# Two changes of order in the softmax pipeline of a windowed-attention stage: the row maximum ahead of the row sum on VectorE, and later slots for the steps behind

## The chip, the cores and the metric

The kernel runs on the 8 cores of one Trainium2 chip. Every core does the same work on its own 2048 tokens; nothing passes between cores. The time is that of the slowest core, in device microseconds (us).

## What is computed

One "macaron" layer on x of 16384 tokens by 1024 features: half a mixture-of-experts block, windowed attention, half a mixture-of-experts block again. The change lies in the attention.

```python
x = x + 0.5 * ffn(layernorm(x))          # shared MLP + 15 experts, top 3 of them weighted
x = x + attn(layernorm(x))
x = x + 0.5 * ffn(layernorm(x))

# attn: 16 heads of 64, chunks of 64 queries
q, k, v = x @ Wq.T + bq, x @ Wk.T + bk, x @ Wv.T + bv
k3, v3 = (chunk before, own chunk, chunk after)
scores = einsum('bnqhd,bnkhd->bhnqk', qc, k3) / sqrt(64)
band = (rel >= -32) & (rel <= 32)        # rel: key position less query position
attn = softmax(where(band & inside, scores, -inf))
out  = einsum('bhnqk,bnkhd->bnqhd', attn, v3).reshape(b, s, d) @ Wo.T + bo
```

The dense reference mixture is computed as written: every expert runs on every token, and the weights of the experts that a token did not pick are zero.

## The kernel before

Each core holds its 2048 tokens and 64 more on either side, feature-major, in `R` (fp32), with the normalised copy in `zT` (bf16). The stages follow one another: layer norm, feed-forward, layer norm, attention, layer norm, feed-forward.

The attention (`phase_attn`) handles four quarters of 512 queries each. A quarter has three parts:

1. The projections K, V and Q, as 128x512 and 128x128 matmuls from `zT` and weights in the two buffers `wA` and `wB`. The weights come by four DMAs of 2 MB on GpSimd's queue (line 731).
2. The softmax loop, 16 iterations j: four blocks of 128 queries by four groups of four heads.
3. The output projection (line 1032, weights in `wB`) and its addition to `R` (line 1044). It starts when the last context copy of the loop is done.

Within the softmax loop one iteration goes through eight steps. The names in the right column are those used from here on.

| step | engine, lines | what | name |
|---|---|---|---|
| 1 | TensorE 869 to 885 | mask by an identity matmul, then scores of 4 heads over 256 keys, into the pair of PSUM banks `pQ[j % 2]` | S(j) |
| 2 | VectorE 946, 948, 951 | negated row maximum from the two banks, then the smaller of the two | max(j) |
| 3 | ScalarE 1005, 1007 | exp with the maximum as bias, PSUM to `esc[j % 2]` | exp(j) |
| 4 | VectorE 932, 934, 937 | row sums of `esc`, reciprocal | sum(j) |
| 5 | GpSimd 969 | `atb = esc * rec` | mul(j) |
| 6 | TensorE 896, 897 | 8 transposes of `atb` into PSUM | T(j) |
| 7 | ScalarE 986 | copy of the transposed block to SBUF | cpT(j) |
| 8 | TensorE 913, 916 and ScalarE 994 | context matmuls, and their copy to `ctxT` | C(j), cpC(j) |

The order is written out by hand. Every engine runs its own queue over slots i = 0, 1, 2, ...; in slot i it does the steps that are listed for it, in this order. A step whose j lies outside 0 to 15 becomes a drain and an empty instruction that still counts the semaphore up, so that every slot adds the same number.

| engine | slot i before |
|---|---|
| TensorE | S(i), T(i-2), C(i-3) |
| VectorE | sum(i-1), max(i) |
| GpSimd | mul(i-1) |
| ScalarE | cpT(i-2), cpC(i-3), exp(i) |

There are 19 slots (`NC2 = NIT + 3`). The functions `pe_s`, `pe_t`, `pe_c`, `d1`, `d2`, `g_n`, `a1`, `a2`, `a3` give the semaphore count at which a step of iteration j is done (`d1` the maximum, `d2` the sum, `g_n` the multiplication, `a1` the exp, `a2` and `a3` the two copies). All buffers of the loop are double: S(j) waits for exp(j-2), exp(j) waits for mul(j-2) and sum(j-2), mul(j) for T(j-2), T(j) for cpT(j-2), C(j) for cpC(j-2).

Of the kernel before, what the change touches and what calls it, by code (L numbers as in the profile page):

```python
# [8 lines left out]
BF16 = mybir.dt.bfloat16  # L9
# [4 lines left out]
P = 128  # L14
# [31 lines left out]
def build_program(upto=99, taps=(), aq=4, anit=16, aout=True, acut=99):  # L46
# [49 lines left out]
    with es:  # L96
# [578 lines left out]
        def phase_attn():  # L675
            uid[0] += 1
            u = uid[0]
            with ExitStack() as ps:
# [9 lines left out]
                vbuf = ps.enter_context(nc.sbuf_tensor(f"at_v{u}", [P, 5, D], BF16))  # L688
                qTb = ps.enter_context(nc.sbuf_tensor(f"at_qT{u}", [P, DC, 512], BF16))
                ctxT = ps.enter_context(nc.sbuf_tensor(f"at_cT{u}", [P, DC, 512], BF16))  # L690
                esc = [ps.enter_context(nc.sbuf_tensor(f"at_es{i}{u}", [P, 4, 256], BF16)) for i in range(2)]
                nmx2 = [ps.enter_context(nc.sbuf_tensor(f"at_n2{i}{u}", [P, 2], F32)) for i in range(2)]
                atb = [ps.enter_context(nc.sbuf_tensor(f"at_ab{i}{u}", [P, 4, 256], BF16)) for i in range(2)]
                atT = [ps.enter_context(nc.sbuf_tensor(f"at_aT{i}{u}", [P, 8, P], BF16)) for i in range(2)]
# [11 lines left out]
                for qh in range(aq):  # L706
# [121 lines left out]
                        return pe1 + 3 * j + 1  # L828

                    def pe_t(j):  # L830
                        return pe1 + 3 * (j + 2) + 2

                    def pe_c(j):
                        return pe1 + 3 * (j + 3) + 3

                    def d2(j):
                        return dve1 + 2 * (j + 1) + 1

                    def d1(j):
                        return dve1 + 2 * j + 2  # L840

                    def g_n(j):
                        return gp1 + j + 2

                    def a2(j):
                        return act1 + 3 * (j + 2) + 1

                    def a3(j):
                        return act1 + 3 * (j + 3) + 2

                    def a1(j):
                        return act1 + 3 * j + 3

                    NC2 = NIT + 3
                    act1v, dve1v = s_act.n, s_dve.n

                    if True:
                        @blk.tensor
                        def _(t):
                            t.wait_ge(s_act.h, act1v)  # L860
                            t.wait_ge(s_dve.h, dve1v)
                            for i in range(NC2):
# [23 lines left out]
                                else:  # L886
                                    t.drain()
                                    t.nop().then_inc(s_pe.h, 1)
                                if 0 <= i - 2 < NIT:
                                    j = i - 2  # L890
                                    t.wait_ge(s_gp.h, g_n(j))
                                    if j >= 2:
                                        t.wait_ge(s_act.h, a2(j - 2))
                                    pT = pT2[j % 2]
                                    for sidx in range(4):
                                        t.transpose(pT[:, 2 * sidx, :], atb[j % 2][:, sidx, 0:128], identb[:, :])  # L896
                                        mm = t.transpose(pT[:, 2 * sidx + 1, :], atb[j % 2][:, sidx, 128:256], identb[:, :])
                                        if sidx == 3:
                                            mm.then_inc(s_pe.h, 1)
                                else:  # L900
                                    t.drain()
                                    t.nop().then_inc(s_pe.h, 1)
                                if 0 <= i - 3 < NIT:
                                    j = i - 3
                                    pl, hq = divmod(j, 4)
                                    t.wait_ge(s_act.h, a2(j))
                                    if j >= 2:
                                        t.wait_ge(s_act.h, a3(j - 2))
                                    pC = pC2[j % 2]
                                    for sidx, e in enumerate((0, 2, 1, 3)):  # L910
                                        h = 4 * hq + e
                                        hp = h % 2
                                        t.matmul(pC[hp * HD:(hp + 1) * HD, e // 2, :],
                                                 vbuf[:, pl, h * HD:(h + 1) * HD],
                                                 atT[j % 2][:, 2 * sidx, :], start=True, stop=False)
                                        mm = t.matmul(pC[hp * HD:(hp + 1) * HD, e // 2, :],
                                                      vbuf[:, pl + 1, h * HD:(h + 1) * HD],
                                                      atT[j % 2][:, 2 * sidx + 1, :], start=False, stop=True)
                                        if sidx == 3:
                                            mm.then_inc(s_pe.h, 1)  # L920
                                else:
                                    t.drain()
                                    t.nop().then_inc(s_pe.h, 1)
                        s_pe.n += 3 * NC2

                        @blk.vector
                        def _(v):
                            for i in range(NC2):
                                if 0 <= i - 1 < NIT:
                                    j = i - 1  # L930
                                    v.wait_ge(s_act.h, a1(j))
                                    v.tensor_reduce(out=sro[j % 2][:, 0:2], in_=esc[j % 2][:, 0:2, :],
                                                    axis=AX.X, op=ALU.add)
                                    v.tensor_reduce(out=sro[j % 2][:, 2:4], in_=esc[j % 2][:, 2:4, :],
                                                    axis=AX.X, op=ALU.add)
                                    v.drain()
                                    v.reciprocal(rec[j % 2][:, :], sro[j % 2][:, :])
                                    v.drain()
                                    v.nop().then_inc(s_dve.h, 1)  # L939
                                else:  # L940
                                    v.drain()
                                    v.nop().then_inc(s_dve.h, 1)
                                if 0 <= i < NIT:
                                    j = i
                                    v.wait_ge(s_pe.h, pe_s(j))
                                    v.tensor_reduce(out=nmx2[j % 2][:, 0:1], in_=pQ[j % 2][0][:, :],
                                                    axis=AX.X, op=ALU.max, negate=True)
                                    v.tensor_reduce(out=nmx2[j % 2][:, 1:2], in_=pQ[j % 2][1][:, :],
                                                    axis=AX.X, op=ALU.max, negate=True)
                                    v.drain()  # L950
                                    v.tensor_reduce(out=nmx[j % 2][:, 0:1], in_=nmx2[j % 2][:, :],
                                                    axis=AX.X, op=ALU.min)
                                    v.drain()
                                    v.nop().then_inc(s_dve.h, 1)
                                else:
                                    v.drain()
                                    v.nop().then_inc(s_dve.h, 1)
                        s_dve.n += 2 * NC2

                        @blk.gpsimd  # L960
                        def _(g):
                            for i in range(NC2):
                                if 0 <= i - 1 < NIT:
                                    j = i - 1
                                    g.wait_ge(s_dve.h, d2(j))
                                    if j >= 2:
                                        g.wait_ge(s_pe.h, pe_t(j - 2))
                                    b_ap = rec[j % 2][:, :].unsqueeze(2).broadcast_to((P, 4, 256))
                                    g.tensor_tensor(out=atb[j % 2][:, :, :], in0=esc[j % 2][:, :, :],  # L969
                                                    in1=b_ap, op=ALU.mult)  # L970
                                    g.drain()
                                    g.nop().then_inc(s_gp.h, 1)  # L972
# [5 lines left out]
                        @blk.scalar  # L978
                        def _(s):
                            for i in range(NC2):  # L980
                                if 0 <= i - 2 < NIT:
                                    j = i - 2
                                    s.wait_ge(s_pe.h, pe_t(j))
                                    if j >= 2:
                                        s.wait_ge(s_pe.h, pe_c(j - 2))
# [1 line left out]
                                else:  # L987
                                    s.drain()
                                    s.nop().then_inc(s_act.h, 1)
                                if 0 <= i - 3 < NIT:  # L990
                                    j = i - 3
                                    pl, hq = divmod(j, 4)
                                    s.wait_ge(s_pe.h, pe_c(j))
                                    s.copy(ctxT[:, 2 * hq:2 * hq + 2, pl * P:(pl + 1) * P],
# [4 lines left out]
                                if 0 <= i < NIT:  # L999
                                    j = i  # L1000
                                    s.wait_ge(s_dve.h, d1(j))
                                    if j >= 2:
                                        s.wait_ge(s_gp.h, g_n(j - 2))
                                        s.wait_ge(s_dve.h, d2(j - 2))
                                    s.activation(esc[j % 2][:, 0:2, :], pQ[j % 2][0][:, :],
                                                 AF.Exp, bias=nmx[j % 2][:, 0:1])
                                    s.activation(esc[j % 2][:, 2:4, :], pQ[j % 2][1][:, :],
                                                 AF.Exp, bias=nmx[j % 2][:, 0:1]).then_inc(s_act.h, 1)
                                else:
                                    s.drain()  # L1010
# [157 lines left out]
```

## Time and profile before

| | us |
|---|---|
| median of 4 runs | 5416.4 |
| lowest and highest of them | 4871.3, 5500.51 |
| the profiled execution | 4869.68 |
| its span, first to last instruction of the slowest core (core 7) | 4867.8 |
| spans of the eight cores | 4854.0 to 4867.8 |

| engine | busy us | share of the span |
|---|---|---|
| PE, TensorE matmul | 4264.8 | 88% |
| DVE, VectorE | 1522.2 | 31% |
| ACT, ScalarE | 879.5 | 18% |
| POOL, GpSimd | 281.1 | 6% |

The profile comes from one execution on the slowest core. A view of groups gives, for each line and engine, the count, the busy time and the idle time before it with the instruction that ended it. The timeline gives single instructions: start in us from the span's start, length in us, engine (PEld is the weight load of TensorE), line, operation, output and inputs, and in brackets the idle time before it and what ended it. A "q" behind an engine's name is that engine's instruction queue. The TensorE clock is given as a share of 2.4 GHz, so 0.50 is 1.2 GHz.

### The profile page before, as it was taken

Reading aid. Unit: us, or ns where it says so; the run is one execution under the profiler, and the core shown is the slowest. Engines: PE = TensorE matmul, PEld = TensorE weight load, DVE = VectorE, ACT = ScalarE, POOL = GpSimd, SP = SyncE. Lnnn points to the kernel's source line nnn. Section 1 sums busy time; section 2 is a strip of 40 time slices with the busy share of each in tenths; the row PEclk is TensorE's granted clock in tenths of the full one; section 3 lists DMA queues with packets and bytes.
Section 4 is the critical chain, followed back from the end, with each engine's and each line's share of the span. In section 5 each row is a group of like instructions: output and inputs, shape, how many; then the busy total and the mean of one; then the engine's idle time right before and its main releaser. Section 6 shows DMA issues by size and latency. Waiting matters only on the chain. (4 is left out here: it accounts for less than half of the span.)

```text
span 4867.8 us, 55255 instructions; the slowest of 8 cores (4854.0 to 4867.8 us)
## 1 busy us (share of the span) xinstructions
PE 4264.8 (88%) x21809; PEld 1983.2 (41%) x21809; DVE 1522.2 (31%) x1740; ACT 879.5 (18%) x932; POOL 281.1 (6%) x183
## 2 busy tenths in 40 slices
PE   1399999999999999953777761899999999999998
PEld 0144444444444444421333330344444444444444
DVE  3522222222222222244432346222222222222222
ACT  1111111111111111120333341111111111111111
POOL 0200000000000000002221222000000000000000
PEclk8699999999999999976677765899999999999999
DMA  3322222222222222103124300322222222222221
GB/s 83 71 37 41 40 40 40 40 44 40 40 40 40 40 40 40 20 0 71 35 53 70 53 18 18 54 45 51 40 55 41 44 39 40 39 40 47 49 40 72
DMA packets 98100, 212.78 MB, mean 44 GB/s; under 512 B 3829, under 2 KB 3829, under 8 KB 96050
## 3 DMA queue, kind: packets, MB, share of 16 engines
q0 software_dynamic: 85664, 173.45, 20.5%
q1 hardware_dynamic: 12184, 35.80, 2.2%
q8 instruction: 179, 2.93, 0.2%
q14 instruction: 73, 0.60, 0.0%
HBM read 369.54 MB, written 8.57 MB: 78 GB/s over the span
## 5 line engine op out<-in xcount | busy, mean ns | idle before, releaser
L580 PE MATMUL ff_pA<-zT,ff_w 128*128 128x512 bf16 (+1 forms) x4608 | 959.5, 363 | 7.5 <-DMA ff_w<-sW 7.5
L604 PE MATMUL ff_pA<-ff_g,ff_w 128*128 128x512 bf16 (+1 forms) x4608 | 958.5, 362 | 0.0
L604 PE MATMUL ff_pB<-ff_g,ff_w 128*128 128x512 bf16 (+1 forms) x4608 | 954.6, 361 | 0.0
L580 PE MATMUL ff_pB<-zT,ff_w 128*128 128x512 bf16 (+1 forms) x4608 | 954.4, 361 | 0.0
L658 DVE TENSOR_TENSOR ff_g<-ff_r,ff_c 128x1024 bf16<-128x1024 bf16 (+1 forms) x480 | 340.1, 709 | 1415.6 <-ACT ff_r L643 1415.6
L643 ACT ACTIVATE ff_r<-ff_pA,eb1c 128x1024 bf16<-128x1024 f32 (+1 forms) x240 | 273.6, 1140 | 2303.9 <-PE ff_pA L580 2303.9
L580 PEld LDWEIGHTS ff_pA<-zT,ff_w 128*128 128x128 bf16 x4608 | 430.2, 98 | 495.0 <-issue 15.6
L604 PEld LDWEIGHTS ff_pA<-ff_g,ff_w 128*128 128x128 bf16 x4608 | 429.8, 98 | 488.2 <-issue 10.3
L604 PEld LDWEIGHTS ff_pB<-ff_g,ff_w 128*128 128x128 bf16 x4608 | 428.5, 98 | 485.9 <-issue 6.1
L580 PEld LDWEIGHTS ff_pB<-zT,ff_w 128*128 128x128 bf16 x4608 | 429.0, 98 | 483.7
L667 DVE TENSOR_TENSOR R<-ff_pA,R 128x1024 f32<-128x1024 f32 (+1 forms) x256 | 322.0, 1258 | 618.0 <-PE ff_pA L604 509.4
L667 DVE TENSOR_TENSOR R<-ff_pB,R 128x1024 f32<-128x1024 f32 (+1 forms) x256 | 322.0, 1258 | 601.1 <-PE ff_pB L604 553.7
L643 ACT ACTIVATE ff_r<-ff_pB,eb1c 128x1024 bf16<-128x1024 f32 (+1 forms) x240 | 273.6, 1140 | 581.5 <-PE ff_pB L580 581.5
L534 POOL DMA_DIRECT2D ff_w<-eW x60 | 52.5, 875 | 3409.6 <-PE ff_pB L580 2650.6
L749 PE MATMUL at_S<-zT,at_wA 128*128 128x128 bf16 (+1 forms) x512 | 78.2, 307 | 125.6 <-DMA at_wA<-WkT 104.1
L362 PE MATMUL rt_p<-rWb,zT 128*128 128x15 bf16 x264 | 11.9, 174 | 190.8 <-PEq L1062 91.3
L251 PE MATMUL ln_psA<-zT,ones_col 128*1 128x512 bf16 (+1 forms) x128 | 47.4, 400 | 122.5 <-ACT ln_gsq L231 103.8
L896 PE MATMUL at_T<-identb,at_ab 128*128 128x128 bf16 x256 | 57.9, 301 | 99.4 <-POOLq L972 85.6
L969 POOL TENSOR_TENSOR at_ab<-at_es,at_rc 128x1024 bf16<-128x1024 bf16 x64 | 121.1, 1892 | 269.9 <-DVEq L939 260.4
L749 PEld LDWEIGHTS at_S<-zT,at_wA 128*128 128x128 bf16 x512 | 40.8, 99 | 163.9 <-issue 135.4
L362 PEld LDWEIGHTS rt_p<-rWb,zT 128*128 128x128 bf16 x264 | 9.8, 104 | 193.3 <-issue 193.3
L896 PEld LDWEIGHTS at_T<-identb,at_ab 128*128 128x128 bf16 x256 | 34.6, 138 | 126.3 <-issue 126.3
(123 smaller groups left out, 1768.2 us busy)
## 6 DMA issues: line engine op xcount, KB each, us to landing
ff_w<-eW POOLq DMA_DIRECT2D x60, 2048.0 KB, 14.9
ff_c<-scr_cwt SPq DMA_DIRECT2D x45, 256.0 KB, 3.3
ff_w<-sW POOLq DMA_DIRECT2D x4, 2048.0 KB, 23.3
at_wA<-WkT POOLq DMA_DIRECT2D x4, 2048.0 KB, 15.0
at_wB<-WvT POOLq DMA_DIRECT2D x4, 2048.0 KB, 14.4
at_wA<-WqT POOLq DMA_DIRECT2D x4, 2048.0 KB, 14.5
at_wB<-WoT POOLq DMA_DIRECT2D x4, 2048.0 KB, 14.0
outT<-R SPq DMA_DIRECT2D x2, 4096.0 KB
```

Source lines behind the costliest of these rows:

```text
L251: t.matmul(psA[0:1, 0:tn], ones_col[:, :], zT[:, c, c0 + to: c0 + to + tn], start=st, stop=sp)
L362: mm = t.matmul(prt[:, :], zT[:, c, cl0 + k * P: cl0 + (k + 1) * P], rWb[:, c, :], start=(c == 0), stop=(c == DC - 1))
L534: g.dma_start(wb[m % 3][:, :, :], src.rearrange("(c p) n -> p c n", p=P)).then_inc(s_wm[m % 3].h, 16)
L580: mm = t.matmul(bank[:, to:to + tn], wb[m1 % 3][:, c, dh * P:(dh + 1) * P], zT[:, c, cl0 + ho + to: cl0 + ho + to + tn], start=(c == 0), s ...
L604: mm = t.matmul(bank[:, to:to + tn], wb[m2 % 3][:, dh, do * P:(do + 1) * P], gbuf[:, dh, to:to + tn], start=(dh == 0), stop=last)
L643: s.activation(rbufs[ridx % 2][:, 0:hn], bank[:, 0:hn], AF.Relu, bias=eb1c[:, dh, ei - 1:ei]).then_inc(s_act.h, 1)
L658: v.tensor_tensor(out=gbuf[:, dh, 0:hn], in0=rbufs[ridx % 2][:, 0:hn], in1=cbufs[e % 2][:, 0:hn], op=ALU.mult)
L667: v.tensor_tensor(out=R[:, do, cl0 + ho: cl0 + ho + hn], in0=bank[:, 0:hn], in1=R[:, do, cl0 + ho: cl0 + ho + hn], op=ALU.add)
L749: mm = t.matmul(bank[:, 0:tn], wA[:, c, do * P:(do + 1) * P], zT[:, c, kc0 + to: kc0 + to + tn], start=(c == 0), stop=(c == DC - 1))
L896: t.transpose(pT[:, 2 * sidx, :], atb[j % 2][:, sidx, 0:128], identb[:, :])
L969: g.tensor_tensor(out=atb[j % 2][:, :, :], in0=esc[j % 2][:, :, :], in1=b_ap, op=ALU.mult)
```

## The change

The slot table becomes the following; there are 21 slots (`NC2 = NIT + 5`).

| engine | slot i after |
|---|---|
| TensorE | S(i), T(i-3), C(i-4) |
| VectorE | max(i), sum(i-1) |
| GpSimd | mul(i-2) |
| ScalarE | cpT(i-3), cpC(i-5), exp(i) |

`esc` has three buffers in place of two, so exp(j) waits for mul(j-3) and sum(j-3). VectorE gets two more waits: max(j) for exp(j-2), and sum(j) for mul(j-2). The waits of the other steps keep their form, and the counting functions are moved to fit. No step is added or taken away. Cut to its core:

```diff
-                esc = [... for i in range(2)]
+                esc = [... for i in range(3)]
...
                     def pe_t(j):
-                        return pe1 + 3 * (j + 2) + 2
+                        return pe1 + 3 * (j + 3) + 2
                     def pe_c(j):
-                        return pe1 + 3 * (j + 3) + 3
+                        return pe1 + 3 * (j + 4) + 3
+                    def d1(j):
+                        return dve1 + 2 * j + 1
                     def d2(j):
-                        return dve1 + 2 * (j + 1) + 1
-                    def d1(j):
-                        return dve1 + 2 * j + 2
+                        return dve1 + 2 * (j + 1) + 2
                     def g_n(j):
-                        return gp1 + j + 2
+                        return gp1 + j + 3
                     def a2(j):
-                        return act1 + 3 * (j + 2) + 1
+                        return act1 + 3 * (j + 3) + 1
                     def a3(j):
-                        return act1 + 3 * (j + 3) + 2
+                        return act1 + 3 * (j + 5) + 2
-                    NC2 = NIT + 3
+                    NC2 = NIT + 5
...  tensor
-                                if 0 <= i - 2 < NIT:     # T
-                                    j = i - 2
+                                if 0 <= i - 3 < NIT:
+                                    j = i - 3
-                                if 0 <= i - 3 < NIT:     # C
-                                    j = i - 3
+                                if 0 <= i - 4 < NIT:
+                                    j = i - 4
...  vector: the block of sum(i-1) is moved behind the block of max(i)
                                 if 0 <= i < NIT:
                                     j = i
                                     v.wait_ge(s_pe.h, pe_s(j))
+                                    if j >= 2:
+                                        v.wait_ge(s_act.h, a1(j - 2))
...
+                                if 0 <= i - 1 < NIT:
+                                    j = i - 1
+                                    v.wait_ge(s_act.h, a1(j))
+                                    if j >= 2:
+                                        v.wait_ge(s_gp.h, g_n(j - 2))
+                                    v.tensor_reduce(out=sro[j % 2][:, 0:2], in_=esc[j % 3][:, 0:2, :],
+                                                    axis=AX.X, op=ALU.add)
...  gpsimd
-                                if 0 <= i - 1 < NIT:
-                                    j = i - 1
+                                if 0 <= i - 2 < NIT:
+                                    j = i - 2
...  scalar
-                                if 0 <= i - 2 < NIT:     # cpT
-                                    j = i - 2
+                                if 0 <= i - 3 < NIT:
+                                    j = i - 3
-                                if 0 <= i - 3 < NIT:     # cpC
-                                    j = i - 3
+                                if 0 <= i - 5 < NIT:
+                                    j = i - 5
-                                    if j >= 2:
-                                        s.wait_ge(s_gp.h, g_n(j - 2))
-                                        s.wait_ge(s_dve.h, d2(j - 2))
+                                    if j >= 3:
+                                        s.wait_ge(s_gp.h, g_n(j - 3))
+                                        s.wait_ge(s_dve.h, d2(j - 3))
```

## Rows read from the trace of the kernel before

**Rows 1.** Busy time of each engine (x instructions), TensorE clock, DMA share, GB/s, by stretch

```profile
2340.00:2400.00 60.00, 44.70 (x265) 19.76 (x264) 34.81 (x73) 30.62 (x48) 22.63 (x13) 0.50 0.00 1
2432.00:2456.00 24.00, 18.67 (x128) 9.93 (x128) 0.21 (x1) 8.49 (x17) 0.79 (x1) 1.00 0.50 88
```

**Rows 2.** Waits from 2327 to 2905 us: total us, times, longest

```profile
ACT at_es L1005 <- DVEq L954: 124.2, 56, 3.6
DVE at_sr L932 <- ACT at_es L1007: 100.1, 60, 2.0
```

**Rows 3.** Timeline of one slot of the first quarter: VectorE, GpSimd, ScalarE

```profile
2397.51 0.69 DVE L932 TENSOR_REDUCE at_sr<-at_es 128x2 f32<-128x512 bf16 x1 [1.66 <-ACT at_es L1007]
...
2399.28 0.69 DVE L946 TENSOR_REDUCE at_n<-at_S 128x1 f32<-128x512 f32 x1 [0.24 <-issue]
2399.32 1.89 POOL L969 TENSOR_TENSOR at_ab<-at_es,at_rc 128x1024 bf16<-128x1024 bf16 x1 [3.06 <-DVEq L939]
...
2400.64 0.15 DVE L951 TENSOR_REDUCE at_nm<-at_n 128x1 f32<-128x2 f32 x1
2401.08 0.69 ACT L1005 ACTIVATE at_es<-at_S,at_nm 128x512 bf16<-128x512 f32 x1 [2.04 <-DVEq L954]
...
2402.46 0.69 DVE L932 TENSOR_REDUCE at_sr<-at_es 128x2 f32<-128x512 bf16 x1 [1.66 <-ACT at_es L1007]
...
2402.71 1.01 ACT L986 COPY at_aT<-at_T 128x1024 bf16<-128x1024 bf16 x1 [0.36 <-PE at_T L897]
...
2403.62 0.38 ACT L994 CAST at_cT<-at_C 128x256 bf16<-128x256 f32 x1
```

**Rows 4.** Timeline, TensorE: transposes, next scores, the transposes after them

```profile
2386.70 0.27 PE L896 MATMUL at_T<-identb,at_ab 128*128 128x128 bf16 x1 [1.21 <-POOLq L972]
...
2388.22 0.61 PE L878 MATMUL at_S<-maskb,identb 128*128 128x512 bf16 x1
...
2389.84 0.61 PE L874 MATMUL at_S<-at_kT,at_qT 64*128 64x256 bf16 x2
...
2391.65 0.26 PE L896 MATMUL at_T<-identb,at_ab 128*128 128x128 bf16 x1 [1.20 <-POOLq L972]
```

**Rows 5.** First scores and output projection, first and last quarter: ns min/median/max, starts

```profile
L878 PE MATMUL at_S<-maskb,identb x16: 376/607/609, 2326.9 to 2398.1; 128*128 128x512 bf16 x16
...
L878 PE MATMUL at_S<-maskb,identb x16: 376/607/609, 2810.4 to 2881.7; 128*128 128x512 bf16 x16
...
L1032 PE MATMUL at_S<-at_cT,at_wB x64: 379/379/634, 2415.1 to 2431.0; 128*128 128x512 bf16 x64
...
L1032 PE MATMUL at_S<-at_cT,at_wB x64: 379/379/634, 2898.7 to 2913.4; 128*128 128x512 bf16 x64
```

**Rows 6.** A satisfied wait on VectorE's queue: ns min/median/max

```profile
L931 DVEq EVENT_SEMAPHORE  x2: 21/21/21, 2342.4 to 2347.3; - x2
```

**Rows 7.** Timeline: first scores of the loop, and the third

```profile
2326.86 0.38 PE L878 MATMUL at_S<-maskb,identb 128*128 128x512 bf16 x1 [1.13 <-ACTq L998]
...
2332.69 0.58 PE L878 MATMUL at_S<-maskb,identb 128*128 128x512 bf16 x1 [2.78 <-ACTq L989]
```

**Rows 8.** Timeline: from the last multiplication of the loop to the next quarter

```profile
2409.22 1.89 POOL L969 TENSOR_TENSOR at_ab<-at_es,at_rc 128x1024 bf16<-128x1024 bf16 x1 [3.06 <-DVEq L957]
...
2412.10 0.93 POOL L731 DMA_DIRECT2D at_wA<-WkT  x1 [0.98 <-issue]
...
2415.13 1.44 PE L1032 MATMUL at_S<-at_cT,at_wB 128*128 128x512 bf16 x3 [0.61 <-ACTq L1011]
...
2432.43 1.89 PE L749 MATMUL at_S<-zT,at_wA 128*128 128x512 bf16 x8 [1.08 <-DVEq L1049]
```

**Rows 9.** The page's DMA issues: KB each, median us from issue to landing

```profile
at_wA<-WkT POOLq DMA_DIRECT2D x4, 2048.0 KB, 15.0
```

**Rows 10.** Timeline of the layer norm: VectorE beside a busy and an idle GpSimd

```profile
2218.46 6.83 DVE L301 TENSOR_TENSOR zT<-zT,ln_c 128x2176 bf16<-128x2176 bf16 x1
...
2231.82 2.43 DVE L301 TENSOR_TENSOR zT<-zT,ln_c 128x2176 bf16<-128x2176 bf16 x1
...
2216.26 6.75 POOL L321 TENSOR_TENSOR zT<-R,ln_rb 128x2176 bf16<-128x2176 f32 x1 [0.15 <-issue]
```

More of the change, by code:

```diff
@@ L690, in phase_attn @@
                 ctxT = ps.enter_context(nc.sbuf_tensor(f"at_cT{u}", [P, DC, 512], BF16))
-                esc = [ps.enter_context(nc.sbuf_tensor(f"at_es{i}{u}", [P, 4, 256], BF16)) for i in range(2)]
+                esc = [ps.enter_context(nc.sbuf_tensor(f"at_es{i}{u}", [P, 4, 256], BF16)) for i in range(3)]
                 nmx2 = [ps.enter_context(nc.sbuf_tensor(f"at_n2{i}{u}", [P, 2], F32)) for i in range(2)]
@@ L928, in _ @@
                             for i in range(NC2):
-                                if 0 <= i - 1 < NIT:
-                                    j = i - 1
[L931 to L942, printed above, removed]
                                 if 0 <= i < NIT:
@@ L957, in _ @@
                                     v.nop().then_inc(s_dve.h, 1)
+                                if 0 <= i - 1 < NIT:
[5 more added lines that the diff above has]
+                                                    axis=AX.X, op=ALU.add)
+                                    v.tensor_reduce(out=sro[j % 2][:, 2:4], in_=esc[j % 3][:, 2:4, :],
+                                                    axis=AX.X, op=ALU.add)
+                                    v.drain()
+                                    v.reciprocal(rec[j % 2][:, :], sro[j % 2][:, :])
+                                    v.drain()
+                                    v.nop().then_inc(s_dve.h, 1)
+                                else:
+                                    v.drain()
+                                    v.nop().then_inc(s_dve.h, 1)
                         s_dve.n += 2 * NC2
@@ L962, in _ @@
                             for i in range(NC2):
-                                if 0 <= i - 1 < NIT:
-                                    j = i - 1
+                                if 0 <= i - 2 < NIT:
+                                    j = i - 2
                                     g.wait_ge(s_dve.h, d2(j))
@@ L968, in _ @@
                                     b_ap = rec[j % 2][:, :].unsqueeze(2).broadcast_to((P, 4, 256))
-                                    g.tensor_tensor(out=atb[j % 2][:, :, :], in0=esc[j % 2][:, :, :],
+                                    g.tensor_tensor(out=atb[j % 2][:, :, :], in0=esc[j % 3][:, :, :],
                                                     in1=b_ap, op=ALU.mult)
@@ L1001, in _ @@
                                     s.wait_ge(s_dve.h, d1(j))
-                                    if j >= 2:
-                                        s.wait_ge(s_gp.h, g_n(j - 2))
-                                        s.wait_ge(s_dve.h, d2(j - 2))
-                                    s.activation(esc[j % 2][:, 0:2, :], pQ[j % 2][0][:, :],
+                                    if j >= 3:
+                                        s.wait_ge(s_gp.h, g_n(j - 3))
+                                        s.wait_ge(s_dve.h, d2(j - 3))
+                                    s.activation(esc[j % 3][:, 0:2, :], pQ[j % 2][0][:, :],
                                                  AF.Exp, bias=nmx[j % 2][:, 0:1])
-                                    s.activation(esc[j % 2][:, 2:4, :], pQ[j % 2][1][:, :],
+                                    s.activation(esc[j % 3][:, 2:4, :], pQ[j % 2][1][:, :],
                                                  AF.Exp, bias=nmx[j % 2][:, 0:1]).then_inc(s_act.h, 1)
```

## The prediction

> **What bounds the kernel now.** I read the per-core spans first (all eight within 14 us), then the page's 40 slices, which put the attention in the middle of the span, then busy time by stretch, then the waits of the attention alone, then single instructions. In the profiled execution the loop of a quarter runs from its first scores to the output projection: 2326.9 to 2415.1 in the first quarter, 2810.4 to 2898.7 in the last [rows 5]. That is 88.2 and 88.3 us; with the other two, about 353 us of the span of 4867.8. The change touches nothing outside this 7%.
>
> Inside the loop no engine is busy all the time: in 60 us TensorE is busy 44.70, VectorE 34.81, ScalarE 30.62, GpSimd 22.63, at a granted clock of 0.50, the 1.2 GHz level [rows 1]. So a ring of waits sets the pace. The waits name it: ScalarE's exp waits for VectorE's maximum (124.2 us), VectorE's sum waits for ScalarE's exp (100.1 us) [rows 2]. One turn can be added up [rows 3]: sum starts 2397.51, the maximum behind it 2399.28 (1.77 later), exp 2401.08 (1.80 later), the next sum 2402.46 (1.38 later). 1.77 + 1.80 + 1.38 = 4.95 us. VectorE works 3.5 of it and stands 1.66 before the sum, because max(i), whose scores have long been ready, is queued behind sum(i-1), and that waits for exp(i-1). Over the loop the mean is higher: the third scores start at 2332.69, the sixteenth at 2398.1 [rows 5, 7], 65.4 / 13 = 5.03 us, as some slots are 0.3 longer.
>
> **The change part by part.** *The swap on VectorE* cuts the ring: max(i) no longer stands behind a wait for exp(i-1). What is left, by cycle:
>
> - VectorE's own work: sum 1.77; maximum from 2399.28 to the end of its last step at 2400.79, plus the 0.24 that the row behind a finished step shows, 1.75 [rows 3]. Together 3.52. Two waits are added; a satisfied one takes 0.021 [rows 6], with 0 below and 0.24 (a whole gap) above; I take 0.02 each as they are the same instruction. 3.57 us per slot.
> - TensorE's own work at 1.2 GHz: transposes to the next scores, 2386.70 to 2388.22, is 1.52 with the context matmuls in it. Scores start 2388.22, the last group 2389.84; that group issues for 0.54, and a change of kind of matmul costs 0.13: 2.29. Then transposes could start; now they wait until 2391.65 for GpSimd [rows 4]. 1.52 + 2.29 = 3.81 us per slot.
> - ScalarE's own work: two exps, about 1.28 to 1.38, the copy 1.01, the small copy 0.38, some gaps: 3.0 us [rows 3].
> - The ring S, exp, S of two slots later: scores to transposes 2.29, transposes to their copy about 1.16, to the small copy 0.91, to exp 0.48, exp and hand-over 1.5: 6.3 us for two slots, 3.2 each [rows 3, 4]. ScalarE's slot order puts exp(i) behind cpT(i-3), which waits for T(i-3), which is behind S(i); this is the work queued behind that wait, and it has 0.6 us a slot to spare.
>
> So with TensorE at 1.2 GHz its own queue is the next bound: 3.81 in place of 5.03.
>
> *The later slots and the third `esc`.* In slot i+3 the product mul(i) is ready before TensorE comes to T(i). Counting from S(i): maximum at 2.33, exp at 4.84, sum behind max(i+1) at 7.9, mul at 9.7, done 11.6, GpSimd to TensorE 0.34, 11.95; TensorE comes to T(i) at 3 x 3.81 + 2.29 = 13.7. Cover 1.8 us; with the old distance of two slots T would come at 9.9 and wait 2.0 us, so the shift is what lets the swap pay. exp(i+3) needs mul(i), ready at 11.6; it starts at 11.4 + 4.84 = 16.3. With two buffers it would need it at 12.5, cover only 0.9. The price of the two slots more is four empty steps per engine, worth at most a few tenths of a us a quarter, behind the last real steps.
>
> *One loop added up*, from S(0), TensorE at 1.2 GHz. S(2) at 5.83 as now [rows 7], since it waits for exp(0) and its table load. S(3) 2.3 later, without a wait. S(4) needs exp(2): 2.33 + 1.80 + 1.38 after S(2), 11.4. S(5) at 15.5 (a full slot and 0.3 for the first product). S(15) ten slots later: 15.5 + 38.1 = 53.6. From there exp(15) at 4.84, sum(15) at 6.22, mul(15) 1.81 later (2397.51 to 2399.32) at 8.03, and from mul(15) to the output projection 5.91 as now (2409.22 to 2415.13) [rows 3, 8]: 13.9. Loop 67.5 us in place of 88.2, 20.7 less, 83 over four.
>
> *What is late next.* The K weights of the next quarter are issued behind the loop on GpSimd's queue, 2.9 us after mul(15) starts, land 15.0 later at about 2427.1 and are wanted at 2432.43 [rows 8, 9]. All of these move together with mul(15), so the cover of 5.3 us stays. The V weights wait for the end of the output projection, as now. The output weights were loaded long before. The saving reaches the end whole, because the stages behind follow in order. Sum: 4869.7 - 83 = 4787 us, 1.7% less.
>
> The sum is made against the profiled execution (4869.68). The median of the four runs, 5416.4, lies 11% above it, while the lowest, 4871.3, agrees with it; my number is for a run like the profiled one. By the same ratio, 0.983, the median would go to about 5324, which is no part of my range.
>
> **The rivals.**
>
> *TensorE goes to 2.4 GHz in the loop, and VectorE sets the pace.* For: in the new loop TensorE would be left no wait, against 44.70 of 60 now, and the K projection, busy 18.67 of 24, is held at clock 1.00 [rows 1]. Against: at full clock TensorE would again have a gap of over 1 us in every slot, and at 75% busy the loop now never rises. VectorE comes to max(3) at 5.83 + 2.33 + 1.75 + 1.77 = 11.7, max(15) at 11.7 + 12 x 3.57 = 54.5, sum(15) at 58.1, mul 59.9, output 65.8. 22.4 x 4 = 90 saved: 4780. The Trainium skill (TensorE: Matmul & The Clock Gate, on the clock gate in Part 1) has the gate released by sustained activity; by it this rival would be the forecast. No row here shows this density of work.
>
> *Another hand-over binds, in part.* The ring through ScalarE, with 0.6 us to spare a slot, holds four hand-overs between engines; should it or TensorE's queue come to 4.3 us, twelve slots cost 0.5 each: 6 us a loop, 4811. For: some slots now carry 0.3 us that I can't place. Against: they would have to come on top in every slot.
>
> *GpSimd slows VectorE, and the kernel gets slower.* In the layer norm a VectorE addition beside a busy GpSimd takes 6.83 against 2.43 alone, 2.8 times [rows 10]. Now mul runs beside the maximum, which reads PSUM, and never beside a sum [rows 3]. Should the sums (1.28 of 1.77) take 2.8 times, they gain 2.3 us and VectorE's slot is 5.9. The loop by this bound is 19.4 + 13 x 5.9 = 96.1, 32 us over four more than now: 4901. It decides from a slot of 5.29 us on. Against: mul starts 0.04 after the maximum and lasts 1.89, the maximum's slot is 1.75, so at most 0.2 us overlap a sum; and the slow instruction of the layer norm reads two tensors, the sum one. The Trainium skill (GPSIMD Engine Reference, Key points) names contention for VectorE instructions with two SBUF inputs or in a two-port mode; by it the sum pays nothing, and the layer norm's rows agree with it.
>
> **How the numbers follow.** Chances: forecast, TensorE at 1.2 GHz sets the pace (4787), 0.45; VectorE sets it (4780), 0.35; a partial loss (4811), 0.14; contention (4901), 0.03; anything else 0.03. The first two are one result for the measurement, whose runs tell about 2%. From the unknown costs: each 0.1 us of a slot is 1.3 x 4 = 5 us. Below the second case I allow 10 us for a shorter start or tail, 4770; above, up to the partial loss and 0.3 us a slot, 4825. Faster by over 2% means below 4772, 7.6 us beyond the better case: 0.08. Slower by over 2% needs VectorE slots of over 7 us: 0.02. Within 2%: 0.90.
>
> **What would show it.** Period of the scores 3.8 (or 3.57 with a clock near 1.00) in place of 5.03; loop 66 to 68 us in each quarter; VectorE's wait for exp before the sum gone, in its place a wait of max for the scores (0.3 a slot) if TensorE binds; no wait of T for GpSimd; 686 ns for the sums as now; the K projection still not waiting for its DMA; feed-forward rows unchanged. I am wrong if the scores' period stays over 4.3 us, or if a reduction lengthens.

## The result and the profile after

The changed kernel takes 4796.2 us (median; 4793.8 to 4797.6) against 4871.6 before. The ratio is 0.985, interval 0.983 to 0.986: 1.5% faster. Its profiled execution takes 4794.55 us. Executions in which the cores of a die ran at a lower clock throughout are left out of these and all later numbers, on both sides; the median of 5416.4 at the head of this document contained three of them.

The loops, read as before from the first scores (line 878) and the output projection (now line 1036) of the first and last quarter, ns min/median/max and first and last start:

```profile
L878 PE MATMUL at_S<-maskb,identb x16: 376/607/607, 2326.9 to 2380.0; 128*128 128x512 bf16 x16
...
L878 PE MATMUL at_S<-maskb,identb x16: 376/607/607, 2752.5 to 2805.2; 128*128 128x512 bf16 x16
...
L1036 PE MATMUL at_S<-at_cT,at_wB x64: 379/379/631, 2395.7 to 2411.2; 128*128 128x512 bf16 x64
...
L1036 PE MATMUL at_S<-at_cT,at_wB x64: 379/379/634, 2820.6 to 2837.0; 128*128 128x512 bf16 x64
```

The first loop is 68.8 us and the last 68.1, in place of 88.2 and 88.3 [rows 5]. The four together are 274 us in place of 353: 79 saved. The projections that stand between and behind the loops give 2.6 of it back; most of that is the last output projection, 14.7 us before (2898.7 to 2913.4) and 16.4 now. Another 1.5 or so lies outside the attention: the spans differ by 74.8 us.

Inside the loop, busy time per engine (TensorE, weight load, VectorE, ScalarE, GpSimd), then the granted clock, in 40 us; and the waits from 2327 to 2905 us that answer to [rows 2]:

```profile
2340.00:2380.00 40.00, 39.88 (x241) 17.83 (x240) 30.77 (x66) 26.88 (x42) 19.63 (x12) 0.50 0.01 2
```

```profile
ACT at_es L1009 <- DVEq L942: 40.1, 52, 2.6
...
DVE at_sr L951 <- issue: 18.3, 57, 0.7
...
PE at_T L896 <- POOLq L976: 16.3, 8, 2.7
```

TensorE is busy 99.7% of the time by the profile where it was 74% [rows 1], and at the same 0.50 of its clock. VectorE's wait of 100.1 us for exp is gone from the list; what stands before its sum is 18.3 us of "issue", a gap that no other engine ends. Exp's wait for the maximum is down from 124.2 to 40.1 us.

One slot of the timeline (start, length, engine, line, and in brackets the idle time before):

```profile
2342.37 1.89 POOL L973 TENSOR_TENSOR at_ab<-at_es,at_rc 128x1024 bf16<-128x1024 bf16 x1 [1.84 <-PE at_T L897]
...
2342.39 0.69 DVE L934 TENSOR_REDUCE at_n<-at_S 128x1 f32<-128x512 f32 x1 [0.31 <-PE at_T L897]
...
2342.79 0.61 PE L878 MATMUL at_S<-maskb,identb 128*128 128x512 bf16 x1
...
2344.23 0.69 DVE L951 TENSOR_REDUCE at_sr<-at_es 128x2 f32<-128x512 bf16 x1 [0.31 <-issue]
...
2344.95 0.29 PE L896 MATMUL at_T<-identb,at_ab 128*128 128x128 bf16 x1
...
2346.06 0.69 DVE L934 TENSOR_REDUCE at_n<-at_S 128x1 f32<-128x512 f32 x1 [0.31 <-PE at_T L897]
...
2346.49 0.61 PE L878 MATMUL at_S<-maskb,identb 128*128 128x512 bf16 x1
```

TensorE: scores 2342.79, transposes 2344.95 (2.16 later), next scores 2346.49 (1.54 later), with no idle time between: 3.70 us. VectorE: maximum 2342.39, sum 2344.23 (1.84), next maximum 2346.06 (1.83): 3.67 us. The two queues are level. GpSimd's product starts beside the maximum, and the sums are as long as before (0.69).

### The profile page after: what moved, and what is told of

The parts are those of the page before. It is cut to its first block and busy times, and to the rows that moved or that the text cites. A ratio compares the mean times of both kernels' runs of the same rounds, so it can differ in the third digit from the quotient of the medians.

```text
span 4793.0 us, 55503 instructions; the slowest of 8 cores (4775.8 to 4793.0 us)
## 1 busy us (share of the span) xinstructions
PE 4262.2 (89%) x21809; PEld 1983.3 (41%) x21809; DVE 1522.0 (32%) x1740; ACT 880.4 (18%) x932; POOL 281.1 (6%) x183
## 5 line engine op out<-in xcount | busy, mean ns | idle before, releaser
L534 POOL DMA_DIRECT2D ff_w<-eW x60 | 52.5, 875 | 3410.3 <-PE ff_pB L580 2651.3
L816 DVE TENSOR_TENSOR at_v<-at_S,bvb 128x512 bf16<-128x512 f32 x40 | 27.7, 692 | 162.2 <-PE at_S L763 162.2
L299 DVE TENSOR_TENSOR zT<-R,ln_rb 128x2176 bf16<-128x2176 f32 (+1 forms) x18 | 66.1, 3675 | 36.8 <-DMA ln_c<-scr_rows 35.7
```

The costliest lines, as they stand in the source:

```text
L299: v.tensor_tensor(out=zT[:, c, sl], in0=R[:, c, sl], in1=rbB[:, 0:cln], op=ALU.mult)
L534: g.dma_start(wb[m % 3][:, :, :], src.rearrange("(c p) n -> p c n", p=P)).then_inc(s_wm[m % 3].h, 16)
L816: v.tensor_tensor(out=vbuf[:, kc, nt * 512:(nt + 1) * 512], in0=bank[:, 0:512], in1=bvb[:, nt * 512:(nt + 1) * 512], op=ALU.add)
```

## The experiments

The runs come in three groups (e1 to e4, e5 to e8, e9 to e12), each timed beside the kernel before (4871.7, 4871.3 and 4873.4 us). The times are medians. Across groups a difference of 2 us tells nothing.

| run | what | us | period of the maximum, us |
|---|---|---|---|
| before | | 4871.6 | 5.0 |
| after | both parts | 4796.2 | 3.70 |
| e1 | the swap alone | 4858.0 | 4.95 |
| e2 | the later slots alone | 4877.2 | 5.03 |
| e3 | after, two `esc` | 4793.1 | 3.70 |
| e4 | after, without the added waits | 4790.1 | 3.62 |
| e5 | after, without the mask matmuls | 4791.2 | 3.70 |
| e6 | after, sums over 64 of the 256 keys of each head | 4788.6 | 3.69 |
| e7 | e5 and e6 together | 4742.9 | 2.91 |
| e8 | after, mask matmuls twice | 4805.9 | 3.81 |
| e9 | after, context copy one slot earlier | 4793.7 | 3.72 |
| e10 | e4, sums on ScalarE | 4790.6 | 3.68 |
| e11 | e4, fillers on TensorE | 4796.4 | 3.58 |
| e12 | e10 and e11 | 4784.4 | 3.62 |

The period is that of the maxima 3 to 15, a mean over the four quarters. Where VectorE starts the loop behind TensorE and catches up, it is shorter than that of the scores: in e4 the maxima of the first loop follow at 3.54 us until VectorE has caught up and at 3.70 from then on, while the scores follow at 3.70 all along, as in the changed kernel. The 3.58 of e11 is of the same kind.

### e1 and e2: one part alone

```diff
 e1: VectorE in the new order, with its two added waits; everything else as before
+ slot i: max(i), sum(i-1)
  T(i-2), C(i-3), mul(i-1), cpT(i-2), cpC(i-3), two esc, NC2 = NIT + 3
 e2: VectorE in the old order; everything else as after (the sum keeps its added wait, the maximum has none)
+ T(i-3), C(i-4), mul(i-2), cpT(i-3), cpC(i-5), three esc, NC2 = NIT + 5
  slot i: sum(i-1), max(i)
```

> The maximum goes ahead of the sum on VectorE, but every other step keeps the slot it had before the change, and esc stays double. My theory: the products of slot i-2 come too late for TensorE, which then holds the next scores back. The ring is scores of j+2 to the end of max 2.33 + 1.83, sum to mul 1.81, mul to transposes 2.23, transposes to the scores of j+4 1.54: 9.74 us for two slots, 4.87 per slot against 5.03 before. Loop 84 to 86 us a quarter, whole kernel 4858 (4848 to 4866), T waiting about 1.2 us a slot for GpSimd. Rival: the swap alone is what pays and the later slots only add fill; then the loop is near 70 us and the kernel near 4797.

Measured 4858.0, ratio 0.998 (0.997 to 1.000). The times alone hardly tell this from no gain; the loops do: 84.7 to 85.7 us each, 341 in all in place of 353. The waits of the attention in e1:

```profile
DVE at_n L934 <- PE at_S L874: 140.6, 57, 15.6
...
PE at_T L896 <- POOLq L976: 82.8, 54, 4.6
```

The ring is the expected one. VectorE now waits for scores in nearly every slot (62 of the 140.6 us stand before the first maxima of the quarters, as before the change), because TensorE stands in front of the transposes for GpSimd, 1.5 us at a time (82.8 / 54). The period is 4.95 where 4.87 was expected.

> The later slots and the third esc, with VectorE's order as before the change (sum first, then maximum). My theory: the ring sum, maximum, exp is untouched at 1.77 + 1.80 + 1.38, so the period of the scores stays 4.95 to 5.03 and the kernel stays within 3 us of the kernel before: 4868 to 4874. Rival, that depth of the pipeline is what pays: below 4840.

Measured 4877.2 (4875.6 and 4878.9): no gain, 5 us more than before and 3 above the stated range. The waits of e2:

```profile
ACT at_es L1007 <- DVEq L956: 162.4, 59, 3.6
...
DVE at_sr L934 <- ACT at_es L1009: 96.6, 56, 2.0
```

The ring of [rows 2] is whole: the sum waits 96.6 us for exp as before. The loops are 358 us in all, 5 more. Some 3 of it is the tail: from the last maximum to the output projection it is 11.8 us, against 11.0 before. The rest is the ring: the sum follows exp by 1.45 us, not 1.38, as it has its second wait (see e4), and the slot is 5.02. So the swap alone brings 14 us, the slots alone lose 5, and together they bring 75. The swap takes the ring away, and the later slots are what lets TensorE use it.

### e3 and e9: parts that were not needed

```diff
 e3
- esc ... range(3);  exp(j) waits for mul(j-3), sum(j-3)
+ esc ... range(2);  exp(j) waits for mul(j-2), sum(j-2)
 e9
- cpC(i-5), NC2 = NIT + 5
+ cpC(i-4), NC2 = NIT + 4
```

> The changed kernel with two esc buffers in place of three. In the changed kernel's trace exp(4) starts at 2344.20 and mul(2), which it would then wait for, ends at 2344.26: exp comes 0.3 to 0.4 us later in each slot, but sum(j), the next step, has over 2 us to spare and the scores of j+2 too, so the delay doesn't add up. Expected: same as the changed kernel, 4795 to 4799. Rival, that the third buffer is needed, as my recorded cover of 0.9 us shrinks with the true slot of 3.7: a delay of 0.35 a slot that does add up would give 4797 + 0.35 x 13 x 4 = 4815.

> The changed kernel with the context copy cpC one slot earlier (i-4 in place of i-5, 20 slots), right behind the context matmuls of the same slot. C(i-4) ends about 4.0 us after S(i) starts, and ScalarE comes to it at about 4.2, after the transposed copy: no wait, exp(i) not later. My theory: same as the changed kernel within 2 us, 4795 to 4799; one slot of distance is as good as two. Rival, that exp falls behind C: up to 0.3 a slot, which would show only if exp had no slack: 4810.

4793.1 and 4793.7: both as the changed kernel or a touch below, and 1 to 2 us under the stated ranges. In e3 exp comes later, 2.11 us after its maximum where it was 1.81 (first loop), and the period stays. The third `esc` and the second slot of distance for the context copy bring nothing.

### e4: the price of the added waits

```diff
- v.wait_ge(s_act.h, a1(j - 2))      # before max(j)
- v.wait_ge(s_gp.h, g_n(j - 2))      # before sum(j)
- sro, rec ... range(2), [j % 2]
+ sro, rec ... range(3), [j % 3]
```

> The changed kernel without the two waits added on VectorE: sums and reciprocals get a third buffer, so that exp(j)'s own wait for mul(j-3) covers the sum's, and the maximum's wait for exp(j-2) is already contained in the scores' wait. My theory: each added wait costs 0.07 us (the gap before a reduction is 0.31 now, 0.24 before), so VectorE's slot goes from 3.68 to 3.54, TensorE at 3.70 alone sets the pace, VectorE is no longer a slot behind at the end, and the tail after the last scores falls from 15.7 to about 14.2: 1.5 x 4 = 6 us, 4791 (4787 to 4794). Rival, that the gap of 0.31 has nothing to do with the waits: no change, 4797, with the gap still 0.31.

Measured 4790.1. Two VectorE rows of e4, a sum and the next maximum:

```profile
2359.81 0.69 DVE L947 TENSOR_REDUCE at_sr<-at_es 128x2 f32<-128x512 bf16 x1 [0.24 <-ACT at_aT L986]
...
2361.59 0.69 DVE L932 TENSOR_REDUCE at_n<-at_S 128x1 f32<-128x512 f32 x1 [0.24 <-issue]
```

The gap is 0.24 again, 0.31 with the added wait. A second wait in front of a VectorE instruction costs 0.07 us even when it is long satisfied. VectorE's slot is 3.54 us so, and TensorE's 3.70 alone sets the pace. The loops are 67.5, 66.9, 67.7 and 67.2 us, 1.2 less each than in the changed kernel; the tail from the last scores to the output projection is 14.7 in place of 15.7 (means over the four), since VectorE comes to the last maximum 2.53 us behind its scores and not 3.51 (first loop).

### e5, e6, e7: which engine binds

```diff
 e5, e7
- t.matmul(pQ[j % 2][k], identb, maskb[...], start=True, stop=False)     # both
- score_mm: start=False
+ score_mm: start=True, stop=True
 e6, e7
- in_=esc[j % 3][:, 0:2, :]          in_=esc[j % 3][:, 2:4, :]
+ in_=esc[j % 3][:, 0:2, 96:160]     in_=esc[j % 3][:, 2:4, 96:160]
```

> The changed kernel without the two mask matmuls of each slot (the mask is left out, so attention goes over all 256 keys of the block). TensorE's slot falls from 3.68 by about 1.07 (2 x 0.54 at 1.2 GHz) to 2.6; VectorE's own 3.68 stays. My theory, VectorE and TensorE are level: the period stays 3.68 to 3.73, the loops lose at most 1 us each by a shorter start, kernel 4793 to 4797. Rival, TensorE alone binds: period about 3.1 (ScalarE and the ring through it), 0.6 x 13 x 4 = 31 us less, 4765.

> The changed kernel with sums over 64 of the 256 columns of each head (the softmax's denominators are partial). VectorE's slot falls by about 0.8 us to 2.9; TensorE's stays. My theory, both are level: period 3.68 by TensorE alone, and only the tail is shorter, since VectorE isn't a slot behind at the end: about 2 us a loop, 4788 (4785 to 4792). Rival, VectorE alone binds: period about 3.1, 4765.

> Both of these left out at once: no mask matmuls and sums over 64 columns. If the two engines are level at 3.68, only this one speeds up: TensorE 2.6, VectorE 2.9, ScalarE 3.0, ring through ScalarE near 3. Period 3.0 to 3.2, saving 0.5 to 0.65 a slot, 26 to 34 us by the slots and up to 8 by start and tail: 4760 (4753 to 4772). Should the period stay at 3.6, another limit was hidden under both, for instance GpSimd's product at 1.9 with its hand-overs.

4791.2 (2 us under the stated range), 4788.6 and 4742.9. Taking 1.07 us (twice the 0.54 from one mask matmul to the next instruction) from TensorE's slot leaves the period where it was; so does taking 0.8 from VectorE's; taking both brings it to 2.91. The same 30 us of the loop (2345 to 2375) in e5, e6 and e7, columns as above:

```profile
2345.00:2375.00 30.00, 17.25 (x163) 10.72 (x164) 23.45 (x49) 20.60 (x34) 15.14 (x8) 0.50 0.00 1
```

```profile
2345.00:2375.00 30.00, 28.58 (x179) 13.53 (x180) 17.15 (x49) 19.66 (x32) 15.48 (x9) 0.50 0.01 2
```

```profile
2345.00:2375.00 30.00, 20.78 (x196) 13.02 (x196) 21.29 (x62) 25.57 (x42) 19.22 (x11) 0.50 0.01 2
```

In e5 TensorE is busy 17.25 of 30 and VectorE as much as in the changed kernel; in e6 the other way round. Either one alone holds the period: VectorE's slot of 3.67 comes to 3.70 on average, as one or two slots of a loop are 0.35 longer. In e7 ScalarE is the busiest with 25.57 of 30, but it isn't what sets the pace: it waits for TensorE's transposes in nearly every slot (25.2 us in 55 waits over the four loops), and TensorE for GpSimd (52.2 us in 59). VectorE has only the gaps of its double waits left:

```profile
2355.29 0.69 DVE L930 TENSOR_REDUCE at_n<-at_S 128x1 f32<-128x512 f32 x1 [0.31 <-issue]
...
2357.12 0.29 DVE L947 TENSOR_REDUCE at_sr<-at_es 128x2 f32<-128x128 bf16 x1 [0.31 <-ACT at_aT L986]
...
2358.16 0.69 DVE L930 TENSOR_REDUCE at_n<-at_S 128x1 f32<-128x512 f32 x1 [0.31 <-issue]
```

Maximum to maximum is 2.87 us: the 3.67 of the changed kernel less the 0.8 by which the two sums are shorter. So e7 too runs at VectorE's pace. It was 10 us faster than the low end of what was expected, which had ScalarE bind at 3.0; ScalarE's own slot is below 2.87.

### e8: more columns, and the clock

```diff
- t.matmul(pQ[j % 2][k], identb, maskb[...], start=True, stop=False)
+ for _k in range(2):
+     t.matmul(pQ[j % 2][k], identb, maskb[...], start=True, stop=(_k == 0))
```

> The changed kernel with each mask matmul issued twice (the second overwrites the first): two more 128x512 matmuls a slot, 1024 more columns, to see whether TensorE's clock leaves 1.2 GHz. If it stays, TensorE's slot is 3.68 + 2 x 0.43 = 4.54 and the kernel 0.86 x 13 x 4 = 45 us slower, 4841 (4836 to 4848), granted clock 0.50. Rival, the denser columns raise the clock to 2.4 GHz: TensorE's slot falls under VectorE's 3.68 and the kernel stays at 4790 to 4800 with a clock near 1.00 in the loop.

Measured 4805.9, only 10 us more than the changed kernel. Two stretches of the first loop of e8:

```profile
2340.00:2350.00 10.00, 9.67 (x56) 3.89 (x53) 6.89 (x14) 4.72 (x7) 5.44 (x3) 0.50 0.00 0
2360.00:2380.00 20.00, 15.08 (x128) 6.24 (x126) 15.78 (x32) 13.38 (x22) 10.85 (x6) 1.00 0.01 2
```

The rival was right, but for the first part of each loop. After some slots in which TensorE has hardly any idle time (9.67 of 10 us busy), the clock goes from 1.2 to 2.4 GHz and stays there to the end of the loop, with TensorE busy 15.08 of 20; in each of the other loops, too, it is down first and up by the second half. Until it rises, the maxima follow each other at up to 4.56 us (first loop, from the third on); afterwards VectorE's pace of 3.67 binds. In the changed kernel TensorE is just as busy by the profile (39.88 of 40), and once down, at its third scores, the clock stays at 1.2 GHz to the end of the loop.

### e10, e11, e12: towards a better version

```diff
 e10, e12 (on e4)
- two exps of 512 columns; two sums on VectorE
+ for k in range(4): s.activation(esc[j % 3][:, k, :], ..., AF.Exp, ..., accum_out=sro[j % 3][:, k:k + 1])
 e11, e12 (on e4)
+ for _k in range({1: 24, 2: 8}.get(i, 0)):      # TensorE, behind S(i)
+     t.matmul(pC2[0][:, :, :], identb[:, :], maskb[:, 1, 0:256], start=True, stop=True)
```

> On top of the kernel without the two added waits: the row sums are taken by ScalarE as it writes exp (four activations of 256 columns, each with its own sum), and VectorE keeps only the reciprocal. VectorE's slot falls from 3.54 to about 2.1, ScalarE's rises from 3.0 to about 3.3 (4 x 0.38 for 2 x 0.64, and a drain). TensorE at 1.2 GHz still needs 3.68: the period stays, only the tail is shorter by 1.3: 4785 (4781 to 4790). Rival, that a sum taken on ScalarE costs 0.2 or more per activation: ScalarE's slot 4.1, 0.4 x 13 x 4 = 22 us slower than without it, 4812.

> On top of the kernel without the two added waits: 24 and 8 filler matmuls of 256 columns (into a bank that the first context overwrites) in TensorE's slots 1 and 2, where it otherwise stands 2.8 us for the first exp and its clock goes from 2.4 to 1.2 GHz. If the clock is kept and then holds with TensorE busy about two thirds of the slot: TensorE's slot 2.4, VectorE's 3.54 binds, a shorter start, 2 to 4 us a loop: 4778 (4772 to 4784), clock near 1.00 in the loop. Rival, that the clock falls all the same: 4789 to 4792, clock 0.50, as without the fillers.

> Both: fillers and ScalarE's sums. If the clock stays at 2.4 GHz, TensorE 2.4, VectorE 2.1, ScalarE 3.3 binds: period 3.3, 0.35 x 13 x 4 = 18 us less than the fillers alone: 4762 (4755 to 4772). If the clock falls, TensorE's 3.68 binds and it is the same as with the sums alone: 4785.

e10 missed: 4790.6, the same as e4. A sum on ScalarE isn't as cheap as I took it; each brings an instruction of its own, 0.22 us in the median (e10, two ScalarE rows):

```profile
2354.60 0.49 ACT L1001 ACTIVATE at_es<-at_S,at_nm 128x256 bf16<-128x256 f32 x1
2354.97 0.21 ACT L1001 ACTIVATION_READ_ACCUMULATOR at_es<-at_S,at_nm 128x1 f32 x1
```

The four exps follow at 0.45 us, 1.8 in place of 1.28. The tail behind the last maximum is shorter by 1.1 (11.2 for 12.3), but the last maximum comes 0.9 later, by a slower start and TensorE's full period.

e11 missed too: 4796.4 for an expected 4778. Two stretches of its first loop:

```profile
2335.00:2350.00 15.00, 11.92 (x86) 6.19 (x86) 11.55 (x24) 8.26 (x11) 5.34 (x3) 1.00 0.00 1
2355.00:2380.00 25.00, 24.89 (x149) 10.71 (x146) 20.23 (x42) 17.58 (x29) 13.26 (x7) 0.50 0.01 2
```

The fillers carry the clock over the gap, and for the first slots TensorE works at 2.4 GHz, busy 11.92 of 15. Then the clock falls within the loop, behind waits of at most 1.26 us, and stays down. The maxima to the output projection take 65.4 us a loop, 0.4 less than in e4, so the attention is no longer than in e4. Of the 6 us by which the kernel is behind e4, 5 lie ahead of the attention, where nothing was changed: in the slowest core's trace the first K projection starts at 2275.6 us, in that of e4 at 2270.5. Within one execution the cores differ there by more (2260.7 to 2275.6 in e11, 2256.4 to 2270.5 in e4). What moved it stays open.

e12, both together, is the fastest kernel here whose work is whole: 4784.4 us, 12 less than the changed kernel and 6 less than e4. It misses its 4762, since the clock holds in some cores and not in others. The same stretch of core 1 and of core 4, the slowest:

```profile
2350.00:2380.00 30.00, 19.93 (x198) 10.02 (x197) 14.40 (x36) 27.81 (x90) 17.03 (x9) 1.00 0.01 2
```

```profile
2350.00:2380.00 30.00, 28.55 (x175) 13.22 (x178) 12.97 (x32) 26.13 (x86) 15.46 (x9) 0.50 0.01 2
```

Core 1 keeps 2.4 GHz in every loop, with TensorE busy two thirds of the time and ScalarE in front (27.81 of 30), and its maxima follow at 3.37 us in the second quarter (2467.9 to 2518.5 for fifteen). Core 4 has 1.2 GHz and 3.53 (2470.7 to 2523.7). Its span is 4784.0, that of core 1 4773.8. The time of the kernel is the slowest core's, so what core 1 shows can't be counted on.

## Why the prediction was right or wrong

The time lay in the range (4770 to 4825), 9 us above the 4787 that was forecast. By the profiled executions 75 us were saved where 83 were forecast. The mechanism was right; what failed is the size of a term.

The step that failed is the term behind the last scores, "From there exp(15) at 4.84" and so on to 13.9. It measured 15.7, 16.4, 15.5 and 15.4 us in the four loops, 7.4 more than forecast in all. It was added up as if VectorE were waiting for TensorE, with 0.24 us to spare in each slot (3.57 against 3.81). The slots are 3.67 and 3.70, so there is nothing to spare, and VectorE comes to the last maximum 3.51 us behind its scores (first loop) and not 2.33. Under that lies the price of the added waits, "a satisfied one takes 0.021", which is 0.07 each: without them the tail is 14.7 (e4). The shorter slots gave 3.4 back (S(15) at 53.1 and 52.5 to 52.7, not 53.6). The projections, which were put at no change, took 2.6 more, and some 1.5 lies outside the attention. 83 - 7.4 + 3.4 - 2.6 - 1.5 is 75.

The chances failed in another way. They spoke only of 2% either way, with 0.90 on a change within that, and called that what a measurement can tell. This was too coarse: the interval is 0.3% wide, and a gain of 1.5% stands clear of no change.

- **The ring.** Right. Sum, maximum and exp in series set the pace (e2 keeps it at 5.03), and the swap cut it.
- **The later slots.** Right in what they are for: with the old distance T was to wait 2.0 us for GpSimd; e1 shows 1.5, and only 14 of the 75 us. The third `esc` was given a cover of 0.9 us by the old slot of 3.81; it is not needed at all (e3), since exp has room to come later.
- **TensorE's own slot.** 3.81 forecast, 3.70 measured. The term was scores to transposes, 2.29; it is 2.16, with nothing for the change of kind of matmul (0.13 assumed).
- **VectorE's own slot.** 3.57 forecast, 3.67 measured, of which 3.54 is there without the added waits (e4). The length of the wait's own row is not its price: the gap in front of the reduction grows by 0.07 for each, within the bound of 0.24. So the case in which TensorE alone binds and the one in which VectorE does came out as one: the two are level (e5, e6, e7), and each alone would hold the period.
- **The tail.** Its rows in the first loop of the changed kernel:

```profile
2380.00 0.61 PE L878 MATMUL at_S<-maskb,identb 128*128 128x512 bf16 x1
...
2385.32 0.69 ACT L1009 ACTIVATE at_es<-at_S,at_nm 128x512 bf16<-128x512 f32 x1 [0.69 <-DVEq L942]
...
2387.33 0.69 DVE L951 TENSOR_REDUCE at_sr<-at_es 128x2 f32<-128x512 bf16 x1 [0.45 <-issue]
...
2389.39 1.89 POOL L973 TENSOR_TENSOR at_ab<-at_es,at_rc 128x1024 bf16<-128x1024 bf16 x1 [0.34 <-DVEq L945]
...
2395.67 1.86 PE L1036 MATMUL at_S<-at_cT,at_wB 128*128 128x512 bf16 x4 [0.80 <-ACTq L1015]
```

  The last exp starts 5.32 after the scores, not 4.84, because a level VectorE is behind TensorE by the end. The last sum starts at 7.33, not 6.22, as VectorE has the sum before it to do first. The last product starts at 9.39, not 8.03: GpSimd comes to it straight from the product before (0.34 idle). From there it is 6.28, not 5.91, as two slots of transposes, copies and context matmuls are still to be run. Together 1.7 us in this loop.
- **The rest of the kernel.** I had it unchanged. The projections took 2.6 us more. The K weights kept their cover: issued 2392.41, 15.0 to land, wanted at 2412.65.
- **The rival with TensorE at 2.4 GHz** (0.35). It did not happen, though TensorE was left no wait: the clock stays at 0.50 with TensorE busy 39.88 of 40 us. In e8, with two more 512-column matmuls in each slot, it rises. The Trainium skill (TensorE: Matmul & The Clock Gate, Part 1) has the clock released by sustained activity; by the busy share of the profile, the changed kernel doesn't bear that out.
- **A hand-over that binds in part** (0.14). The ring through ScalarE never showed up, not even in e7 at 2.91 us a slot.
- **GpSimd slowing VectorE** (0.03). Didn't happen: sums 0.69 before and after, the product 1.89. The rule of the Trainium skill (GPSIMD Engine Reference, Key points), that GpSimd contends with VectorE instructions that have two SBUF inputs or run in a two-port mode, agrees, for the little overlap that there is.
- **Slots that are 0.35 longer.** They are still there: in the changed kernel, too, exp and the sum sometimes start 0.35 later behind a maximum. What causes them stays open.

## What to carry to other kernels

When engines take turns by a hand-written order, add up one turn of the ring before looking at any engine's load: here no engine was over 75% busy, and swapping two steps on one queue removed the wait. But a swap needs distance for the steps behind it: alone it was worth 14 us, with one slot more for the product and its transposes 75. When the next engine has little to spare, add up the tail with that engine behind, too. Once the ring is gone, check whether two engines are level, since then relief for either one alone brings almost nothing.

## What the runs showed of the hardware

- A wait that is already satisfied costs VectorE 0.07 us when a second one stands in front of the same instruction, over three times the 0.021 of its own row.
- TensorE's granted clock doesn't follow the busy share of the profile: 0.50 at 39.88 of 40 us busy (changed kernel), 1.00 at 15.08 of 20 (e8), and in e11 a fall from 1.00, at 11.92 of 15, to 0.50 behind waits of at most 1.26 us. In e12 the eight cores, with the same program, part: some hold 2.4 GHz through a loop and some don't.
- A row sum taken along with exp on ScalarE adds a read instruction of 0.19 to 0.24 us (e10); four of 256 columns follow each other at 0.45 us.
